# Loading the input first and the weights in six groups, with the semaphores set on ScalarE and the derived tables made in a new order

## The chip, the core and the metric

The kernel runs on one core of one Trainium2 chip. The metric is the device time of one execution in microseconds (us), and each version is timed in several runs. A core has five engines that run their own instruction streams and wait for one another through semaphores: TensorE (PE), VectorE (DVE), ScalarE (ACT), GpSimd (POOL) and SyncE (SP), which here issues every transfer between HBM and the core's memory (DMA).

## What is computed

Two transformer layers over 16 sequences of 256 tokens with 128 features. Each layer adds an attention and a feed-forward result, both taken from the same normalised input, to the running value:

```python
x = L0_attn_x
xn = _layernorm(x, axis=-1)
x = x + _L0_attn_ref(xn, ...) + _L0_ffn_ref(xn, ...)
xn = _layernorm(x, axis=-1)
x = x + _L1_attn_ref(xn, ...) + _L1_ffn_ref(xn, ...)
```

`_L0_attn_ref` is causal attention with random exponential features (16 heads of 8). `_L0_ffn_ref` is a block of depth 2 with windowed attention (8 heads of 64, rotary tables `cos`, `sin` and a scale that depends on the position), a normalisation and a gated feed-forward each. `_L1_attn_ref` is softmax attention, `_L1_ffn_ref` a mixture of 8 experts plus a shared one. Weights and biases come in as separate inputs. Some are combined before they are used: a normalisation's gain is multiplied into the first feed-forward weight `w1`, its bias is multiplied through `w1` and added to `b1`, the head scales are multiplied into the rotary tables.

## The kernel before

One program does everything. The batches are taken two at a time, so there are 8 turns (`TURNS`) of `for it in range(TURNS)` on every engine, and each turn does both layers for 512 tokens. All weights (9.7 MB) stay in the core's memory for the whole program. What lies ahead of the turns, here called the prologue, runs once, and that is all that the change touches.

The five engines' parts are written by hand in program order, and each waits with `wait_ge(semaphore, count)`. The counts of a turn start at `COUNTS[name] * (it + 1)`, so that each of the 116 semaphores in `COUNTS` is first raised by its own count: `sp.sem_inc(sem[n], COUNTS[n])` (L408), 116 instructions that stand in SP's stream ahead of its first transfer.

The prologue before the change, engine by engine:

- SP: 116 semaphore instructions (L408), then 31 weight and table transfers (L412) that all raise one semaphore, `loaded`, then the input of turn 0, `x_in` (L413).
- POOL waits for all of `loaded` (L449), then clears or fills eight tiles (L450 to L459) and counts them in `started`.
- DVE waits for `loaded` and `started` (L1256, L1257). It makes the derived tables, counted in `prep`: `fbias`, `projblk`, `sqblk`, the 16 pieces of `rot` (L1274), `apb`, the scaled `w1s` (L1282), `b1s`, three rows of `rows`, and the centred second half of `w1s` (L1291, which copies what PE made). Only then it takes the moments of the input and normalises it to `xn` (L1345 to L1359).
- PE waits for `loaded` and for DVE's memset (`prep_ps`), makes the bias products (L500, 24 instructions, and L506, 8), then multiplies the second `w1` by `center` (L511), waits for all tables (`prep` 14), and then goes into turn 0: it transposes `xn` (L520, `turn_input`), makes two value tiles (L541, `early_value`), the queries and keys (L534, `favor_query`) and the values (L549, `favor_values`). The first matmul of the loop over turns is L669.
- ACT waits for `prep` 14 and `started` 9, then copies the transposed input to `hT` and `xnT` (L1077 to L1084), the value tiles (L1089) and the scaled queries (L1103).

Of the kernel before, what the change touches and what calls it, by code (L numbers as in the profile page):

```python
# [7 lines left out]
ALU = mybir.AluOpType  # L8
ACT = mybir.ActivationFunctionType
# [54 lines left out]
    "stack_in": 26 * 16, "nm_out": 16, "nm_in": 32,  # L64
}
# [61 lines left out]
def build(nc, w, x, out):  # L127
    with ExitStack() as ctx:
# [5 lines left out]
        loaded = ctx.enter_context(nc.semaphore("weights_loaded"))  # L134
# [246 lines left out]
        def bank_of(name, k=0):  # L381
            return bank[AT[name, k][0]]
# [62 lines left out]
        N_LOADS = len(W)  # L445

        @block.gpsimd
        def _(pool):
            pool.wait_ge(loaded, 16 * N_LOADS)  # L449
# [42 lines left out]
        def _(pe):  # L492
            mm = nc.tensor.matmul
            pe.wait_ge(loaded, 16 * N_LOADS)
            pe.wait_ge(prep_ps, 1)

            for l in range(DEPTH):
                for c, (o, m) in enumerate(HC):
                    for g in range(2):
                        last = mm(bank[0][0:m, 6 * l + 2 * c + g:6 * l + 2 * c + g + 1],  # L500
                                  W["w1"][:, l, g * HID + o:g * HID + o + m], W["cols"][:, 14 + 1 + l:16 + l],
                                  start=True, stop=True)
            for i, weights in enumerate((W["fw"], W["aw"])):
                for side in range(2):
                    c = 19 + 2 * i + side
                    last = mm(bank[3][:, i * D:(i + 1) * D], W["cols"][:, c:c + 1].broadcast_to([P, P]), weights[:, 3 + side, :],  # L506
                              start=(side == 0), stop=(side == 1), skip_group_check=True)
            last.then_inc(prep_ps, 1)
            pe.wait_ge(prep, 11)
            for g in range(2):  # L510
                last = mm(bank[1 + g][:, 0:HID], W["center"][:], w1s[:, 1, g * HID:(g + 1) * HID], start=True, stop=True)  # L511
            last.then_inc(prep_ps, 1)
            pe.wait_ge(prep, 14)
            pe.wait_ge(started, 9)
            I = W["ident"]
# [55 lines left out]
            pe.wait_ge(sem["favor_qk"], COUNTS["favor_qk"] + 2)  # L571
            favor_values(0)
            for it in range(TURNS):
# [69 lines left out]
                for l in range(DEPTH):  # L643
# [166 lines left out]
                    for b in range(G):  # L810
# [443 lines left out]
        def _(dve):  # L1254
            V = nc.vector
            dve.wait_ge(loaded, 16 * N_LOADS)  # L1256
            dve.wait_ge(started, 9)  # L1257
            done = [0]

            def made(ins):  # L1260
                done[0] += 1
                ins.then_inc(prep, 1)


            V.memset(bank[0][:, 0:12], 0.0).then_inc(prep_ps, 1)
            made(V.tensor_scalar(fbias[:], W["cols"][:, 0:2], FD ** -0.5, None, ALU.mult))
            made(V.tensor_tensor(projblk[:].rearrange("p (a m) -> p a m", a=4),
                                 W["projT"].unsqueeze(1).broadcast_to([P, 4, FM]),
                                 W["block8"].rearrange("p (a m) -> p a m", a=4), ALU.mult))
            made(V.tensor_scalar(sqblk[:], W["block8"], -0.5, None, ALU.mult))  # L1270
            for l in range(DEPTH):
                for qk in range(2):
                    for i, (trig, half) in enumerate(((0, 0), (1, 1), (0, 1), (1, 0))):
                        ins = V.tensor_scalar(rot[:, l, qk, i, :], W["rotary"][:, 2 * qk + trig, :],  # L1274
                                              W["cols"][:, 2 + 4 * l + 2 * qk + half:3 + 4 * l + 2 * qk + half],
                                              None, ALU.mult)
                    made(ins)
            made(V.tensor_scalar(apb[:, 0:1], W["cols"][:, 17:18], AD ** -0.5, None, ALU.mult))
            made(V.tensor_copy(apb[:, 1:2], W["cols"][:, 18:19]))
            dve.wait_ge(prep_ps, 2)  # L1280
            for l in range(DEPTH):
                made(V.tensor_scalar(w1s[:, l, :], W["w1"][:, l, :], W["cols"][:, 10 + l:11 + l], None, ALU.mult))  # L1282
            made(V.tensor_tensor(b1s[:, :], bank[0][:, 0:12], W["b1"][:], ALU.add))
            assert done[0] == 12, done
            V.tensor_tensor(W["rows"][:, 3, :], W["rows"][:, 3, :], W["rows"][:, 6, :], ALU.add)
            for i, r in enumerate((1, 5)):
                V.tensor_tensor(W["rows"][:, r, :], bank[3][:, i * D:(i + 1) * D], W["rows"][:, r, :], ALU.add)
            made(V.memset(mv[:], 1.0))
            dve.wait_ge(prep_ps, 3)
            for g in range(2):  # L1290
                ins = V.tensor_copy(w1s[:, 1, g * HID:(g + 1) * HID], bank[1 + g][:, 0:HID])  # L1291
            made(ins)

# [76 lines left out]
            link(V.memset(ra[:, 0:TT], 1.0))  # L1370
            input_moments(0)
            link(rsqrt(2 * TT))
            input_root()
            input_scale(0)
            for it in range(TURNS):
                now, prior, freed = counters(dve, it)
                def favor_out(b):
# [16 lines left out]
                for l in range(DEPTH):  # L1394
                    for p, (qk, g) in enumerate(PAIRS):
# [340 lines left out]
```

## Time and profile before

| | |
|---|---|
| Median of three runs | 2192.03 us (2189.34 to 2197.23) |
| The profiled execution, its own time | 2193.24 us |
| Its span, first to last instruction | 2191.5 us |
| PE, DVE, ACT, POOL busy | 84%, 61%, 35%, 12% of the span |
| Mean granted TensorE clock | 0.952 |

The span is what the trace covers, and all positions below are microseconds from its start. Busy shares are averages over 8 turns and say nothing about the first 80 us, where the change lies; for these the chain of waits and the order in time are to be read. In the stretches of the prologue the page's column for the granted clock prints 1.00, whatever PE does there.

### The profile page before, as it was taken

How to read it: one execution, taken by the hardware profiler on the slowest of the kernel's cores; microseconds unless marked ns; L12 is line 12 of the kernel's file. 1: busy time of each engine (PE TensorE's matmuls, PEld its weight loads, DVE VectorE, ACT ScalarE, POOL GpSimd, SP SyncE). 2: the span in 40 equal slices, each digit the busy share in tenths (PEclk: the TensorE clock that was granted, in tenths of full speed). 3: DMA queues.
4: the chain of work that ended last, by engine and by line, in shares of the span. 5: the costliest groups of instructions: out<-in, count | busy, mean ns of one | idle time of the engine just before them, and what ended most of it. 6: DMA issues, size and time to landing. Idle time of an engine off the chain costs nothing.

```text
span 2191.5 us, 43331 instructions
## 1 busy us (share of the span) xinstructions
PE 1835.0 (84%) x18116; PEld 1061.8 (48%) x18116; DVE 1335.9 (61%) x2752; ACT 765.2 (35%) x1441; POOL 272.2 (12%) x222
## 2 busy tenths in 40 slices
PE   1698898988988889878888888888897988988887
PEld 1254454554544644536445454454553554545544
DVE  1567546765476745767547675476656675467754
ACT  0323433324533235323352232623425223433234
POOL 0101101101021010110210102101011011012010
PEclk9999999999999989999999999999999999999999
DMA  4000200002000020000200001000100002000010
GB/s 177 1 7 2 28 4 6 6 2 30 2 11 1 2 29 6 8 1 2 29 7 7 1 9 23 7 7 1 19 14 6 7 2 29 2 6 1 3 29 7
DMA packets 27477, 29.77 MB, mean 14 GB/s; under 512 B 3525, under 2 KB 25845, under 8 KB 26741
## 3 DMA queue, kind: packets, MB, share of 16 engines
q1 hardware_dynamic: 27284, 27.01, 6.3%
q8 instruction: 145, 2.38, 0.5%
q14 instruction: 48, 0.39, 0.1%
HBM read 12.06 MB, written 2.36 MB: 7 GB/s over the span
## 4 chain that ended last, share of the span: by engine, by line
PE 52%; DVE 28%; ACT 7%; issue 5%; DMA 4%; SPq 4%; POOL 0%; ACTq 0%; DVEq 0%
PE bank L957 5%; PE bank L731 5%; PE bank L947 4%; PE bank L932 4%; DMA phi<-parts 3%; SPq L430 3%; DVE ls L1455 3%; DVE ftm L1381 2%; PE bank L763 2%; PE bank L970 2%; ACT phi L1246 2%; DVE lc L1437 2%; ACT lc L1246 2%; PE bank L669 2%; DVE parts L1391 2%
## 5 line engine op out<-in xcount | busy, mean ns | idle before, releaser
L1622 DVE TENSOR_REDUCE amx<-bank 128x2 f32<-128x512 f32 x256 | 163.1, 685 | 98.4 <-PE bank L970 98.4
L1212 ACT ACTIVATE silu<-bank 128x512 f32<-128x512 f32 x144 | 84.1, 595 | 298.0 <-PE bank L932 286.0
L1610 DVE TENSOR_TENSOR mh<-bank,silu 128x512 f32<-128x512 f32 x144 | 99.5, 692 | 123.4 <-PE bank L947 115.1
L957 PEld LDWEIGHTS bank<-w_mw,mh 128*128 128x128 f32 x1152 | 145.2, 202 | 24.4 <-issue 24.4
L957 PE MATMUL bank<-w_mw,mh 128*128 128x128 f32 x1152 | 153.2, 289 | 0.0
L1641 DVE RECIPROCAL ftm<-bank 128x512 f32<-128x512 f32 x16 | 53.7, 3358 | 154.4 <-PE bank L1053 154.4
L485 POOL TENSOR_TENSOR xB<-xn2T,lsq 128x512 f32<-128x512 f32 x32 | 40.7, 1273 | 812.1 <-ACT lsq L1218 812.1
L932 PE MATMUL bank<-xn2T,w_mw 128*128 128x512 f32 x288 | 141.1, 612 | 0.0
L1455 DVE RECIPROCAL ls<-bank 128x256 f32<-128x256 f32 x64 | 112.2, 1753 | 39.7 <-PE bank L783 39.6
L1443 DVE TENSOR_REDUCE lmx<-bank 128x4 f32<-128x512 f32 x128 | 79.5, 685 | 89.4 <-PE bank L731 89.4
L669 PE MATMUL bank<-hT,w_wqkv 128*128 128x512 f32 x256 | 119.0, 602 | 11.9 <-ACT lsq L1123 6.2
L466 POOL TENSOR_TENSOR lc<-lc,ls 128x512 f32<-128x512 f32 x32 | 40.9, 1278 | 639.6 <-DVE lc L1413 639.6
L731 PE MATMUL bank<-lc 32*64 32x128 f32 (+1 forms) x3072 | 104.4, 334 | 0.0
L731 PEld LDWEIGHTS bank<-lc 32*64 32x64 f32 (+1 forms) x3072 | 78.5, 181 | 32.0 <-issue 20.3
L763 PE MATMUL bank<-lc 32*128 32x192 f32 (+1 forms) x2048 | 88.1, 308 | 0.0
L1437 DVE TENSOR_TENSOR lc<-lc,bank 128x512 f32<-128x512 f32 x128 | 79.1, 680 | 13.6 <-PE bank L712 13.6
L763 PEld LDWEIGHTS bank<-lc 32*128 32x128 f32 x2048 | 75.9, 185 | 14.5 <-issue 12.1
L1407 DVE TENSOR_TENSOR lc<-bank,rot 128x512 f32<-128x512 f32 x64 | 43.9, 687 | 60.5 <-PE bank L669 60.5
L669 PEld LDWEIGHTS bank<-hT,w_wqkv 128*128 128x128 f32 x256 | 45.4, 190 | 70.9 <-issue 44.7
L970 PE MATMUL bank<-lc,phi 48*128 48x256 bf16 x512 | 50.0, 286 | 34.1 <-DMA phi<-parts 34.1
L719 PE MATMUL bank<-w_winmask,w_ident 128*128 128x512 bf16 x128 | 47.7, 449 | 35.3 <-DVE lc L1437 14.3
L1123 ACT ACTIVATE lsq<-bank 128x512 f32<-128x512 f32 x64 | 36.5, 596 | 115.5 <-DVE ls L1410 69.2
(284 smaller groups left out, 3678.1 us busy)
## 6 DMA issues: line engine op xcount, KB each, us to landing
phi<-parts SPq DMA_DIRECT2D x96, 64.0 KB
lc<-parts SPq DMA_DIRECT2D x96, 64.0 KB
w_mw<-in_mw SPq DMA_DIRECT2D x3, 1152.0 KB
x_in<-in_x SPq DMA_DIRECT2D x8, 256.0 KB, 2.7
out<-res SPq DMA_DIRECT2D x8, 256.0 KB, 2.3
w_wqkv<-in_wqkv SPq DMA_DIRECT2D x1, 1536.0 KB
w_w<-in_w SPq DMA_DIRECT2D x1, 682.0 KB
mh<-in_rotary SPq DMA_DIRECT2D x1, 512.0 KB
```

The costliest lines, as they stand in the source:

```text
L669: mm(bank_of("loc_raw", n)[:], W["wqkv"][:, l, c * P:(c + 1) * P], h, start=True, stop=True).then_inc(sem["loc_raw_ps"], 1)
L731: ins = mm(bank_of("loc_max", k + i)[u * WIN:u * WIN + m, c0:c0 + P], lc[r, c, q0 + u * WIN:q0 + u * WIN + m], lc[r, 4 + c, k0:k0 + P], st ...
L763: mm(bank_of("loc_sT", 4 * k + i)[:, c0:c0 + nq], lc[r, 4 + c, t + kt * P:t + kt * P + P], lc[r, c, t + q0:t + q0 + nq], start=False, stop ...
L932: mm(bank_of("moe_g", n)[:], W["mw3"][:, ORDER[q], i * P:(i + 1) * P], xn2T[:], start=True, stop=True).then_inc(sem["moe_g_ps"], 1)
L947: mm(bank_of("moe_u", n)[:], W["mw1"][:, ORDER[q], i * P:(i + 1) * P], xw[q % 2] if q else xn2T[:], start=True, stop=True).then_inc(sem["m ...
L957: last = mm(bank_of("final")[:, t], mh[:, (2 * q + i) % 4, t], W["mw2"][:, ORDER[q], i, :], start=(q == 0 and j == 0 and i == 0), stop=Fal ...
L970: ins = mm(o[:, qt * SEQ:(qt + 1) * SEQ], qst[r, hh, t + qt * P:t + qt * P + P], kst[r, hh, t:t + SEQ], start=True, stop=True)
L1246: A(apr[k % 8], bank_of("att_sT", k)[:], ACT.Exp).then_inc(sem["att_p"], 1)
L1437: V.tensor_tensor(lc[:, c, :], lc[:, c, :], bank_of("loc_rb", m)[:], ALU.mult).then_inc(sem["loc_qk"], 1)
L1455: V.reciprocal(lrec[:, k % 2, :], bank_of("loc_den", k)[:, 0:SEQ]).then_inc(sem["loc_rec"], 1)
L1610: V.tensor_tensor(mh[:, n % 4, :], bank_of("moe_u", n)[:], silu[:, n % 2, :], ALU.mult).then_inc(sem["moe_h"], 1)
L1622: V.tensor_reduce(amx[:, 2 * b:2 * b + 2, h], bank_of("att_max", n)[:].rearrange("p (t k) -> p t k", t=2), AX.X, ALU.max).then_inc(sem["at ...
```

## The change

Five things change, all in the prologue.

1. `x_in` is SP's first transfer, and the weights follow in six groups, in a new order; each group raises its own semaphore (`loaded_first`, `loaded_gated`, `loaded_favor`, `loaded_local`, `loaded_tables`, `loaded_rest`). The weight `wqkv` is split into its two layers, which go into different groups.
2. Each engine waits for a group where it first needs it. POOL waits for no load at all.
3. The 116 semaphore instructions move from SP to ACT, in reversed order.
4. ACT runs one `Exp` on a single column once `started` is reached, so that its table load stands ahead of the first copy.
5. DVE normalises the input first and makes the tables after it, in a new order. PE transposes the input first and makes the bias products after it, in `bank6` instead of `bank0` and `bank3`; the centring matmul moves behind `favor_query`.

```diff
+LOADS = {
+    "first": ("ident", "cols"),
+    "gated": ("w1", "b1", "center"),
+    "favor": ("fw", "aw", "block8", "projT"),
+    "local": ("rotary", "wqkv0", "rows"),
+    "tables": ("sumrow", "causal", "sumcol", "ident4", "headrow", "winmask", "nmrow", "bandmask", "den", "mean"),
+    "rest": ("wo", "w2", "wqkv1", "wr", "rb", "pick", "rank", "mw3", "mw1", "mw2"),
 }
...
+        def arrived(group):
+            return loaded[group], 16 * len(LOADS[group])
...
-            for n in COUNTS:
-                sp.sem_inc(sem[n], COUNTS[n])
+            sp.dma_start(x_in[:], x[0]).then_inc(x_in_sem, 16)
+            for group, names in LOADS.items():
+                for n in names:
...
             sp.sem_inc(stored, 16)
-            for n, ap in w.items():
-                if n != "ones2":
-                    sp.dma_start(W[n] if n in ("rotary", "block8", "projT") else W[n][:], ap).then_inc(loaded, 16)
-            sp.dma_start(x_in[:], x[0]).then_inc(x_in_sem, 16)
...
-            pool.wait_ge(loaded, 16 * N_LOADS)
...
-            pe.wait_ge(loaded, 16 * N_LOADS)
-            pe.wait_ge(prep_ps, 1)
...
-            pe.wait_ge(prep, 14)
-            pe.wait_ge(started, 9)
...
+            def bias_products():
+                pe.wait_ge(*arrived("gated"))
+                pe.wait_ge(prep_ps, 1)
...
+                pe.wait_ge(*arrived("favor"))
...
+                last.then_inc(prep_ps, 1)
+
+            def centred_weights():
+                pe.wait_ge(prep, 5)
+                for g, o in enumerate((bank_of("xnT"), bank_of("loc_v", 0))):
+                    last = mm(o[:, 0:HID], W["center"][:], w1s[:, 1, g * HID:(g + 1) * HID], start=True, stop=True)
+                last.then_inc(prep_ps, 1)
...
+            pe.wait_ge(started, 9)
+            pe.wait_ge(*arrived("first"))
             turn_input(0)
+            bias_products()
             pe.wait_ge(sem["xnT"], COUNTS["xnT"] + 1)
+            pe.wait_ge(*arrived("local"))
             for j in range(EARLY):
                 early_value(0, j)
...
             pe.wait_ge(sem["favor_qk"], COUNTS["favor_qk"] + 2)
+            centred_weights()
             favor_values(0)
+            pe.wait_ge(prep, 13)
+            pe.wait_ge(*arrived("tables"))
...
+                    if it == 0 and l == 0:
+                        pe.wait_ge(*arrived("rest"))
                     for b in range(G):
                         n = 2 * l + b
                         pe.wait_ge(*freed("loc_wo", n))
...
-            act.wait_ge(prep, 14)
+            for n in reversed(COUNTS):
+                act.sem_inc(sem[n], COUNTS[n])
             act.wait_ge(started, 9)
+            A(warm[:], phibias[:], ACT.Exp)
...
+            act.wait_ge(prep, 1)
             queries(0)
+            act.wait_ge(prep, 13)
...
+            dve.wait_ge(prep_ps, 2)
+            dve.wait_ge(*arrived("favor"))
+            dve.wait_ge(*arrived("gated"))
+            made(V.tensor_scalar(sqblk[:], W["block8"], -0.5, None, ALU.mult))
...
+            dve.wait_ge(*arrived("local"))
+            tables(0)
...
+            tables(1)
+            dve.wait_ge(prep_ps, 3)
```

What stands in the streams, first of SP, whose rows are transfers (tile, source, shape). Before, the small tables come first and the input last:

```order
L412 DMA w_ident<-in_ident 128x128
L412 DMA w_ident4<-in_ident4 128x512
...
L412 DMA mh<-in_rotary 128x1024
...
L412 DMA w_wqkv<-in_wqkv 128x3072
...
L412 DMA w_mw2<-in_mw2 128x2304
L413 DMA x_in<-in_x 128x4x128
```

Now:

```order
L420 DMA x_in<-in_x 128x4x128
L427 DMA w_ident<-in_ident 128x128
L427 DMA w_cols<-in_cols 128x23
L427 DMA w_w1<-in_w1 128x1364
...
L427 DMA mh<-in_rotary 128x1024
L425 DMA w_wqkv<-in_wqkv 128x1536
...
L427 DMA w_mw2<-in_mw2 128x2304
```

The input moved from the 32nd place to the first, and the first half of `wqkv` and the rotary tables from the middle to places 11 and 12; the three largest weights (`mw`) still stand last.

PE at its start, before (L500 and L506 are the bias products, L511 the centring, L520 the input's transposes, L541, L534 and L549 the first products of turn 0, L669 the loop):

```order
L500 MATMUL bank0<-w_cols,w_w1 128x1 [waits bias_products,weights_loaded]
...
L506 MATMUL bank3<-w_fw,w_cols 128x128 x2
...
L511 MATMUL bank1<-w_w1,w_center 128x341 [waits vector_prepared]
...
L520 MATMUL bank2<-w_ident,xn 128x128 [waits glu_as,xn,pool_prepared,vector_prepared]
...
L541 MATMUL bank3<-w_wqkv,hT 128x512 [waits glu_gs,hT,xnT]
...
L534 MATMUL bank7<-xnT,w_fw 128x512 [waits att_mx,xnT,loc_v]
...
L549 MATMUL bank7<-w_fw,xnT 128x128 [waits att_o,favor_qk]
...
L669 MATMUL bank0<-hT,w_wqkv 128x512 [waits loc_v,favor_qk,att_p,xnT,hT]
```

And now (L535 the transposes, L515 and L522 the bias products, L556, L549 and L564 the first products, L529 the centring, L691 the loop):

```order
L535 MATMUL bank2<-w_ident,xn 128x128 [waits glu_as,xn,loaded_first,pool_prepared]
...
L515 MATMUL bank6<-w_cols,w_w1 128x1 [waits bias_products,loaded_gated]
...
L522 MATMUL bank6<-w_fw,w_cols 128x128 [waits loaded_favor]
...
L556 MATMUL bank3<-w_wqkv,hT 128x512 [waits hT,glu_gs,loaded_local,xnT]
...
L549 MATMUL bank7<-xnT,w_fw 128x512 [waits att_mx,xnT,loc_v]
...
L529 MATMUL bank2<-w_w1,w_center 128x341 [waits vector_prepared,favor_qk]
...
L564 MATMUL bank7<-w_fw,xnT 128x128 [waits att_o]
...
L691 MATMUL bank0<-hT,w_wqkv 128x512 [waits favor_qk,xnT,loc_v,hT,att_p,loaded_tables,vector_prepared]
```

The transposes moved ahead of the bias products and the centring behind the queries; the wait for all tables moved from the transposes to the loop's first matmul.

DVE at its start, before:

```order
L1265 MEMSET bank0 128x12 [waits pool_prepared,weights_loaded]
L1266 TENSOR_SCALAR fbias<-w_cols 128x2
...
L1274 TENSOR_SCALAR rot<-mh,w_cols 128x256 x16
...
L1282 TENSOR_SCALAR w_w1<-w_w1,w_cols 128x682 [waits bias_products]
...
L1291 COPY w_w1<-bank1 128x341 [waits bias_products]
L1291 COPY w_w1<-bank2 128x341
L1370 MEMSET ra 128x4
L1345 BN_STATS st_in<-x_in 128x6 [waits x_loaded,vec_step]
```

And now:

```order
L1286 MEMSET bank6 128x12 [waits pool_prepared]
L1363 MEMSET ra 128x4
L1338 BN_STATS st_in<-x_in 128x6 [waits x_loaded,loaded_first,vec_step]
...
L1352 TENSOR_SCALAR xn<-x_in,mv_in,rs_in 128x128 [waits vec_step]
...
L1389 TENSOR_SCALAR sqblk<-mh 128x128 [waits loaded_gated,loaded_favor,bias_products]
...
L1378 TENSOR_SCALAR rot<-mh,w_cols 128x256 [waits loaded_local]
L1378 TENSOR_SCALAR rot<-mh,w_cols 128x256 x7
...
L1378 TENSOR_SCALAR rot<-mh,w_cols 128x256 x8
L1405 COPY w_w1<-bank2 128x341 [waits bias_products]
L1405 COPY w_w1<-bank3 128x341
L1445 TENSOR_TENSOR lc<-bank0,rot 128x512 [waits loc_raw_ps,att_pv,vector_prepared,loaded_tables]
```

The input's statistics and scaling moved ahead of all tables, and the copies of the centred weight (L1405) stand last, just ahead of the loop's first instruction (L1445).

## Rows read from the trace of the kernel before

**Rows 1.** Core's span and mean granted clock.

```profile
core 0: 2191.5 us, clock 0.952
```

**Rows 2.** Busy time by stretch, turns 0 and 1 (PE, PEld, DVE, ACT, POOL; PEclk, DMA share, GB/s).

```profile
76.40:340.80 264.40, 228.51 (x2258) 131.49 (x2257) 162.84 (x337) 95.42 (x181) 33.44 (x26) 0.95 0.06 9
340.80:605.00 264.20, 228.23 (x2263) 131.05 (x2261) 167.82 (x341) 95.46 (x180) 33.45 (x26) 0.95 0.06 10
```

**Rows 3.** The chain that ended last, 0 to 76.5 us: start, duration, what.

```profile
25.59 15.56 DMA w_mw<-in_mw
...
41.20 0.53 POOL hT L450
...
45.77 0.09 DVE fbias L1266
...
45.99 4.69 PE bank L500 x24
50.68 1.93 PE bank L506 x8
52.63 1.07 DVE w_w L1282 x2
...
53.75 2.66 PE bank L511 x4
...
57.36 0.04 DVE ra L1370
...
62.08 1.10 PE bank L520 x4
...
63.28 1.28 ACT L1077
...
66.46 3.79 PE bank L541 x4
...
70.93 3.79 PE bank L534 x4
...
75.48 1.16 PE bank L549 x8
```

**Rows 4.** Line L408, SP's semaphore instructions: ns min/median/max, first and last start.

```profile
L408 SPq EVENT_SEMAPHORE  x116: 17/17/17, 0.7 to 7.9; - x116
```

**Rows 5.** SP's first and last transfer of the prologue, in order of time.

```profile
8.06 0.89 SPq L412 DMA_DIRECT2D w_ident<-in_ident  x2
...
26.88 0.85 SPq L413 DMA_DIRECT2D x_in<-in_x  x1
```

**Rows 6.** Busy time by stretch while the weights load (columns as in Rows 2).

```profile
8.00:16.00 8.00, 0.00 (x0) 0.00 (x0) 0.00 (x0) 0.00 (x0) 0.00 (x0) 1.00 0.47 129
...
20.00:36.00 16.00, 0.00 (x0) 0.00 (x0) 0.00 (x0) 0.00 (x0) 0.00 (x0) 1.00 1.01 407
36.00:41.00 5.00, 0.00 (x0) 0.00 (x0) 0.00 (x0) 0.00 (x0) 0.00 (x0) 1.00 0.51 192
```

**Rows 7.** Tile `x_in` in the prologue, and line L419 (later turns): issue to landing.

```profile
DMA to landing us min/median/max: 14.9/14.9/14.9
DMA to landing us min/median/max: 2.5/2.7/4.7
```

**Rows 8.** DMA packets by size from 16 to 18 us, and from 36 to 40 us.

```profile
DMA packets 111, 0.45 MB, mean 227 GB/s; under 512 B 0, under 2 KB 0, under 8 KB 111
...
DMA packets 587, 0.95 MB, mean 237 GB/s; under 512 B 31, under 2 KB 511, under 8 KB 511
```

**Rows 9.** In order of time: start, duration, engine, line, tiles.

```profile
46.18 4.29 DVE L1274 TENSOR_SCALAR rot<-mh,w_cols 128x256 f32<-128x256 f32 x16
...
76.48 1.88 PE L669 MATMUL bank<-hT,w_wqkv 128*128 128x512 f32 x4
...
80.22 3.70 PE L669 MATMUL bank<-hT,w_wqkv 128*128 128x512 f32 x8
...
137.25 1.97 PE L815 MATMUL bank<-mh,w_wo 128*128 128x256 f32 x8
```

More of the change, by code:

```diff
@@ L64 @@
     "stack_in": 26 * 16, "nm_out": 16, "nm_in": 32,
+}
+LOADS = {
[5 more added lines that the diff above has]
+    "rest": ("wo", "w2", "wqkv1", "wr", "rb", "pick", "rank", "mw3", "mw1", "mw2"),
 }
@@ L133, in build @@
         sem = {n: ctx.enter_context(nc.semaphore(n)) for n in COUNTS}
-        loaded = ctx.enter_context(nc.semaphore("weights_loaded"))
+        loaded = {g: ctx.enter_context(nc.semaphore("loaded_" + g)) for g in LOADS}
         prep = ctx.enter_context(nc.semaphore("vector_prepared"))
@@ L493, in _ @@
             mm = nc.tensor.matmul
-            pe.wait_ge(loaded, 16 * N_LOADS)
-            pe.wait_ge(prep_ps, 1)
[L497 to L511, printed above, removed]
@@ L512, in _ @@
-            last.then_inc(prep_ps, 1)
-            pe.wait_ge(prep, 14)
-            pe.wait_ge(started, 9)
-            I = W["ident"]
+            I = W["ident"]
+            def bias_products():
+                pe.wait_ge(*arrived("gated"))
+                pe.wait_ge(prep_ps, 1)
+                for l in range(DEPTH):
+                    for c, (o, m) in enumerate(HC):
+                        for g in range(2):
+                            mm(bank[6][0:m, 6 * l + 2 * c + g:6 * l + 2 * c + g + 1],
+                               W["w1"][:, l, g * HID + o:g * HID + o + m], W["cols"][:, 14 + 1 + l:16 + l],
+                               start=True, stop=True)
+                pe.wait_ge(*arrived("favor"))
+                for i, weights in enumerate((W["fw"], W["aw"])):
+                    for side in range(2):
+                        c = 19 + 2 * i + side
+                        last = mm(bank[6][:, (1 + i) * D:(2 + i) * D], W["cols"][:, c:c + 1].broadcast_to([P, P]),
+                                  weights[:, 3 + side, :], start=(side == 0), stop=(side == 1), skip_group_check=True)
+                last.then_inc(prep_ps, 1)
@@ L1255, in _ @@
             V = nc.vector
-            dve.wait_ge(loaded, 16 * N_LOADS)
             dve.wait_ge(started, 9)
[L1258 to L1292, printed above, removed]
+            V.memset(bank[6][:, 0:12], 0.0).then_inc(prep_ps, 1)
             step = [0]
@@ L1370, in _ @@
             link(V.memset(ra[:, 0:TT], 1.0))
+            dve.wait_ge(*arrived("first"))
             input_moments(0)
@@ L1374, in _, with made, tables @@
             input_scale(0)
+            done = [0]
+            def made(ins):
+                done[0] += 1
+                ins.then_inc(prep, 1)
+            def tables(l):
+                for qk in range(2):
+                    for i, (trig, half) in enumerate(((0, 0), (1, 1), (0, 1), (1, 0))):
+                        ins = V.tensor_scalar(rot[:, l, qk, i, :], W["rotary"][:, 2 * qk + trig, :],
+                                              W["cols"][:, 2 + 4 * l + 2 * qk + half:3 + 4 * l + 2 * qk + half],
+                                              None, ALU.mult)
+                    made(ins)
@@ new lines, in _ @@
+            made(V.tensor_scalar(fbias[:], W["cols"][:, 0:2], FD ** -0.5, None, ALU.mult))
+            made(V.tensor_scalar(apb[:, 0:1], W["cols"][:, 17:18], AD ** -0.5, None, ALU.mult))
+            made(V.tensor_copy(apb[:, 1:2], W["cols"][:, 18:19]))
+            dve.wait_ge(prep_ps, 2)
+            dve.wait_ge(*arrived("favor"))
+            dve.wait_ge(*arrived("gated"))
+            made(V.tensor_scalar(sqblk[:], W["block8"], -0.5, None, ALU.mult))
+            for l in (1, 0):
+                made(V.tensor_scalar(w1s[:, l, :], W["w1"][:, l, :], W["cols"][:, 10 + l:11 + l], None, ALU.mult))
@@ new lines, in _ @@
+            made(V.tensor_tensor(projblk[:].rearrange("p (a m) -> p a m", a=4),
+                                 W["projT"].unsqueeze(1).broadcast_to([P, 4, FM]),
+                                 W["block8"].rearrange("p (a m) -> p a m", a=4), ALU.mult))
+            dve.wait_ge(*arrived("local"))
+            tables(0)
+            V.tensor_tensor(b1s[:, :], bank[6][:, 0:12], W["b1"][:], ALU.add)
+            V.tensor_tensor(W["rows"][:, 3, :], W["rows"][:, 3, :], W["rows"][:, 6, :], ALU.add)
@@ new lines, in _ @@
+            for i, r in enumerate((1, 5)):
+                V.tensor_tensor(W["rows"][:, r, :], bank[6][:, (1 + i) * D:(2 + i) * D], W["rows"][:, r, :], ALU.add)
+            made(V.memset(mv[:], 1.0))
+            tables(1)
+            dve.wait_ge(prep_ps, 3)
+            for g, o in enumerate((bank_of("xnT"), bank_of("loc_v", 0))):
+                ins = V.tensor_copy(w1s[:, 1, g * HID:(g + 1) * HID], o[:, 0:HID])
+            made(ins)
+            assert done[0] == 13, done
+            dve.wait_ge(*arrived("tables"))
@@ L1375, in _ @@
             for it in range(TURNS):
                 now, prior, freed = counters(dve, it)
+                if it == 0:
+                    dve.wait_ge(prep, 13)
                 def favor_out(b):
@@ L1394, in _ @@
                 for l in range(DEPTH):
+                    if it == 0 and l == 1:
+                        dve.wait_ge(*arrived("rest"))
                     for p, (qk, g) in enumerate(PAIRS):
```

7 lines of the change are left out of this document (6 added, 1 removed).

## The prediction

> **What bounds the kernel now.** I read first the core's span and clock [rows 1], then the turns [rows 2]. Two turns take 264.4 and 264.2 us. Eight such turns are 2114 of the 2191.5 us, and no instruction of a turn is changed apart from two waits for a weight group in turn 0. So the change can only act on what lies ahead of the loop's first matmul, which starts at 76.48 [rows 9]. There the chain of waits is to be read [rows 3]: for the first 41 us it holds only SP's issue and the transfers, the last of them a `mw` weight, of the experts in the second layer. POOL's fills follow (41.20), then PE's bias products, DVE's scaling and PE's centring, then the input's normalisation (57.36), the transposes (62.08), ACT's copies with a table load (63.28), the value tiles, the queries and the loop. One engine works at a time, and each row on this chain is worth its full length. The reader is to see that the question is not how busy an engine is, but which of these rows still stand on the chain afterwards.
>
> **What starts earlier.** SP's 116 semaphore instructions run from 0.7 to 7.9 us [rows 4], and the first transfer follows at 8.06 [rows 5]; so SP can now issue at 0.7. One issue takes about (26.88 - 8.06) / 31 = 0.6 us, and 0.45 while little is queued (0.89 for two [rows 5]). `x_in` alone lands 2.5 to 4.7 us after its issue in the later turns [rows 7]: by 3.4 here, 5.4 at worst. `ident` and `cols` are issued by 1.6 and land by some 5. POOL waits for nothing and starts with the program, at about 0.7 (where L408 starts), and its fills took 45.77 - 41.20 = 4.57 us [rows 3], so DVE may start at 5.2.
>
> **The new chain, summed.**
> - POOL's fills: 0.67 + 4.57 = 5.2.
> - DVE: a memset of under 0.1, then from the memset of `ra` to PE's first transpose 62.08 - 57.36 = 4.72: 10.1.
> - PE transposes: 1.10 and a step of 0.05: 11.2.
> - PE bias products, now behind the transposes: 52.63 - 45.99 = 6.64: 17.9. ACT's copies lie beside them: from the table load's end at 63.28 + 1.28 to 66.46, 1.9 after 11.2, so 13.1. The table load (1.28) is off the chain, if ACT is ready in time (below).
> - value tiles to the end of the queries: 75.48 - 66.46 = 9.02: 26.9.
> - centring, now behind the queries: 2.66 at the pace of [rows 3]. At that place PE changed its pace before: four matmuls L541 take 3.79 [rows 3], eight L669 of the same form 3.70 a few us later [rows 9], half as long each. The granted-clock column prints 1.00 in both stretches, so I go by the durations; 2 to 1 is what its levels of 2.4 and 1.2 GHz would give. At this pace the centring is 1.3. I take 1.3, since just this row lies behind the same two steps as before: 28.2, with 29.6 as the other end.
> - DVE's two copies: from the centring's end at 53.75 + 2.66 to 57.36, about 1 us, beside `favor_values` on PE (1.16 [rows 3]): 29.4.
> The loop starts at 29.4 instead of 76.48: 47.1 us less. Gone from the chain are the wait for all loads and SP's semaphores (40.5 of it), DVE's scaling (1.07), the table load (1.28), the copies to `hT` and `xnT` (1.9), half of the centring (1.3) and the overlap of the last copies (about 1).
>
> **What I cost at nothing, and its cover.**
> DVE's tables now lie between the bias products (17.9) and the centring's end (28.2). They are 16 pieces for 4.29 us [rows 9], the scaling 1.07, and small ones (about 1.5, an estimate from 11 small instructions, most of them shorter than the 0.27 of one of the 16 pieces): 6.9 in all, done at 24.8. Behind them wait the copies, which need the centring anyway. Cover left: 3.4 us. Centring itself needs only the scaling, ready at 19.3.
> ACT's semaphore instructions: at SP's pace of 7.3 us for 116 [rows 4] they end at 8.0, the table load (1.28) at 9.3, and the first copy is wanted at 11.2, so 1.9 us is left. Queued behind them are all of ACT's copies, and every engine that waits for a semaphore raised there; `xn`, which PE needs at 10.1, is the 46th, at 3.6. ACT's own pace isn't in the trace. At twice SP's pace they end at 15.3, the copies at 18.5, and the loop loses 0.6.
> The group `local` (3.5 MB with all ahead of it) is wanted at 17.9. From 20 to 36 us the transfers ran at 407 GB/s [rows 6]; 129 GB/s from 8 to 16 us is the pace of small tables issued one by one. With `x_in` and the small ones done at 3.5, the remaining 3.2 MB take 8 us: 11.5, and the last 5 us before 41 ran at half pace, since single engines were late [rows 6]: 14.3 with that tail. Cover left: 3.6 us.
> `tables` (0.8 MB, small) by about 16, wanted at 29.4. `rest` ends where it did, less 7.4: about 34; its first user is L815 at 137.25 [rows 9], 61 us into the loop, so 90 in the new one.
>
> ACT's table load stands at 1.28 and the three copies fit into the 1.9 us behind it [rows 3], so 1.3 comes off. The Trainium skill (ScalarE: Activation LUTs, What ACT_TABLE_LOAD costs) adds a drain of 1.38 to each switch, 2.66 in all; by that the gain would be 48.4. The trace shows no such gap, though before it ACT had nothing to drain.
>
> **The base.** The profiled execution took 2193.24, 1.2 above the median of 2192.03 and inside the three runs. 2193.24 - 47.1 = 2146.1 for it, 2144.9 against the median. I give 2145.
>
> **Rivals.**
> - PE keeps its slow pace longer: centring 2.66, and the loop's first matmuls too. What was there before PE sped up is 9 us of value tiles and queries with 0.65 between them [rows 3]. The same stands there now, but what counts isn't shown. Price: 1.3 for the centring and up to 2 in the loop: 2146 to 2149.
> - PE speeds up earlier, since bias products and value tiles now follow without a gap: the queries (3.79) would take half, up to 1.9 less, and some of the value tiles: 2141 to 2144. Against it: the 6.6 us of bias products alone did not speed it up before [rows 3].
> - `local` is late. If queued transfers shared the engines instead of going in order, it would land with the last of them, 33.1 us (8.06 to 41.20 [rows 3, 5]) after a start at 0.7: at 33.8, and the loop would start 16 later: 2161. Against it: from 16 to 18 us all 111 packets were of 2 to 8 KB, and from 36 to 40 there came 511 small ones, as `x_in` has, at the very end, where it stood in the queue [rows 8]. A milder form, an engine that is late by more than 3.6 us or instruction fetches of ACT and DVE that stand behind the weights, costs 1 to 6: 2146 to 2151. The Trainium skill (Runtime: NRT & Kernel Launch, Instruction fetch mechanics) lets each engine fetch its instructions in blocks through a DMA queue of its own. By that rule ACT, with 116 instructions more ahead of its first copy, could fetch just while the weights load; no row here shows a fetch under such load, which is why the mild form has more than a token chance.
> - The groups don't help, since one engine still waits for nearly everything ahead of its first work. The first waits in each stream speak against it: POOL has none, DVE and PE begin with `first`. Price, if only SP's 7.3 us were gained: 2184.7.
> - Slower than before: the turns get longer. The granted clock is 0.952 [rows 1], so 2 x 0.048 x 2191.5 = 210 us are spent at 1.2 GHz, the lower level. The turns would begin at another phase of whatever sets this. To eat 47 us and 0.3% (6.6) more, at half a microsecond for each at the lower level, these 210 would have to become 317, a clock of 0.927. Both turns show 0.95 and differ by 0.2 us [rows 2], against the 6.7 per turn that it takes. Then 2199 or more.
>
> **How the numbers follow.** The forecast sum with its own spread of 2 either way 0.55; slow pace longer 0.15; pace earlier 0.12; late transfers or fetches, mild form 0.12; in full 0.02; groups no help 0.01; longer turns 0.01; something that none of these names 0.02, shared between faster and the rest. The range takes the first four but for their ends: 2140 to 2152. A measurement of this kernel tells about 0.3% (6.6 us) from no change. Only the longer turns and half of the unnamed case fall outside of faster: faster 0.97, same 0.015, slower 0.015.
>
> **What would show it.** In the profile after: SP's first transfer at about 0.7; POOL's fills from 0.7 to 5.2; the transposes at 10.1; the bias products right behind, to 17.9, and the value tiles without a gap (a gap released by a transfer means that `local` is late, one released by ACT that its semaphore instructions are); the queries' end at 26.9; the loop's first matmul at 29.4; turns of 264. The prediction is wrong if a turn changes by more than 1 us, if the value tiles start after 20, or if ACT reaches its first copy after 12.

## The result, and the profile after

The changed kernel takes 2139.96 us (median of four runs, 2130.53 to 2142.15) against 2191.22 for the kernel before: a ratio of 0.9761, 95% interval 0.9725 to 0.9798. That is 51.3 us less where 47.1 were forecast, and 2139.96 lies just below the range's lower end of 2140. In a later comparison on another occasion the same two kernels gave 0.9785 (0.9770 to 0.9801, 2139.53 against 2186.6, four and nine runs), 47.1 us less. Two executions among all that were timed for this document lie far outside of the rest (2649.17 and 9517.61 us), and no median or ratio given here counts them. The profiled execution of the changed kernel took 2142.15.

The core's span and mean granted clock:

```profile
core 0: 2140.4 us, clock 0.953
```

Turns 0 and 1 of the changed kernel, busy time by stretch (PE, PEld, DVE, ACT, POOL; PEclk, DMA share, GB/s), to be laid beside [rows 2]:

```profile
25.76:290.10 264.34, 228.19 (x2256) 131.20 (x2256) 163.36 (x337) 95.33 (x180) 33.41 (x26) 0.95 0.07 12
290.10:554.30 264.20, 228.41 (x2273) 131.43 (x2276) 169.11 (x344) 95.66 (x181) 33.41 (x26) 0.95 0.06 10
```

The turns are what they were. From the loop's first matmul to the end it is 2140.4 - 25.76 = 2114.6 us, before 2191.5 - 76.48 = 2115.0. All but 0.4 us of the gain lies ahead of the loop, where the chain of waits now reads (start, duration, what; beside [rows 3]):

```profile
5.26 4.32 DMA mh<-in_projT
...
10.23 1.08 PE bank L535 x4
11.32 4.35 PE bank L515 x24
15.67 1.92 PE bank L522 x8
17.59 2.30 PE bank L556 x4
...
20.56 2.00 PE bank L549 x4
...
22.58 0.70 ACT fqs L1130
...
23.32 1.43 PE bank L529 x4
...
24.78 0.94 DVE w_w L1405 x2
...
25.76 1.98 PE bank L691 x4
```

The reader sees the transposes (L535), the bias products right behind them, the value tiles (L556) without a gap, the queries (L549), the centring (L529), DVE's copies and the loop (L691). The view puts the time from 5.26 to 9.58 down to a transfer (`projT`); DVE's own rows say otherwise. In order of time, and below them the transfer of `cols`, the last of the group `first` (KB, and us from issue to landing):

```profile
5.04 0.10 POOL L472 MEMSET phibias<- 128x1 f32 x1
5.22 0.07 DVE L1286 MEMSET bank<- 128x12 f32 x1 [5.22 <-POOL phibias L472]
...
5.58 0.87 DVE L1338 BATCH_NORM_STATS2 st_in<-x_in 128x6 f32<-128x128 f32 x4 [0.23 <-DVE ra L1363]
...
8.86 1.28 ACT L1100 ACT_TABLE_LOAD   x1 [8.86 <-issue]
```

```profile
w_cols<-in_cols SPq DMA_DIRECT2D x1, 11.5 KB, 3.7
```

POOL's fills end at 5.14 and DVE starts 0.1 us later, on two memsets. Then it stands idle for 0.2 us, until its first statistics at 5.58: `cols`, issued at 1.78, lands at 5.5, and the statistics wait for it. In a second and a third profile of the same kernel (experiment 10) it took 3.4 and 3.1 us, and the statistics start at 5.39, straight behind the memsets. So fills and `cols` end at nearly the same time here, and either can be the last. From there DVE works through to `xn` (L1352). ACT has issued its 116 semaphore instructions by 8.86.

The transfer of `rows`, the last of the group `local`, KB and us from issue to landing:

```profile
w_rows<-in_rows SPq DMA_DIRECT2D x1, 448.0 KB, 7.8
```

`rows` is issued at 6.68, so `local` is complete at 14.5, 3.1 us before its first user.

### The profile page after: what moved, and what is told of

It reads as the page before. It is cut to its first block, busy times and chain, and to the rows that moved or that the text cites. A ratio compares the mean times of both kernels' runs of the same rounds, so it can differ in the third digit from the quotient of the medians.

```text
span 2140.4 us, 43336 instructions
## 1 busy us (share of the span) xinstructions
PE 1829.1 (85%) x18116; PEld 1062.6 (50%) x18116; DVE 1335.0 (62%) x2752; ACT 765.1 (36%) x1442; POOL 271.9 (13%) x222
## 3 DMA queue, kind: packets, MB, share of 16 engines
q8 instruction: 145, 2.38, 0.5%
## 4 chain that ended last, share of the span: by engine, by line
PE 52%; DVE 28%; ACT 7%; issue 4%; SPq 4%; DMA 4%; ACTq 0%; DVEq 0%
PE bank L981 5%; PE bank L753 5%; SPq L446 4%; PE bank L971 4%; PE bank L956 4%; DMA phi<-parts 3%; DVE ls L1493 3%; DVE ftm L1417 3%; PE bank L785 3%; ACT phi L1275 2%; PE bank L994 2%; DVE parts L1427 2%; ACT lc L1275 2%; DVE lc L1475 2%; PE bank L691 2%
## 5 line engine op out<-in xcount | busy, mean ns | idle before, releaser
L691 PE MATMUL bank<-hT,w_wqkv 128*128 128x512 f32 x256 | 119.1, 603 | 12.1 <-ACT lsq L1152 6.2
L785 PEld LDWEIGHTS bank<-lc 32*128 32x128 f32 x2048 | 75.9, 185 | 14.5 <-issue 12.1
L691 PEld LDWEIGHTS bank<-hT,w_wqkv 128*128 128x128 f32 x256 | 45.4, 190 | 71.2 <-issue 44.5
L741 PE MATMUL bank<-w_winmask,w_ident 128*128 128x512 bf16 x128 | 47.0, 444 | 35.7 <-DVE lc L1475 14.5
L956 PEld LDWEIGHTS bank<-xn2T,w_mw 128*128 128x128 f32 x288 | 50.9, 193 | 53.1 <-issue 51.8
```

Source lines behind the costliest of these rows:

```text
L691: mm(bank_of("loc_raw", n)[:], W["wqkv"][:, l, c * P:(c + 1) * P], h, start=True, stop=True).then_inc(sem["loc_raw_ps"], 1)
L785: mm(bank_of("loc_sT", 4 * k + i)[:, c0:c0 + nq], lc[r, 4 + c, t + kt * P:t + kt * P + P], lc[r, c, t + q0:t + q0 + nq], start=False, stop ...
L956: mm(bank_of("moe_g", n)[:], W["mw3"][:, ORDER[q], i * P:(i + 1) * P], xn2T[:], start=True, stop=True).then_inc(sem["moe_g_ps"], 1)
```

## The experiments

Where the loop starts can be read to 0.1 us in a profile, while the time of an execution wanders: from the loop's first matmul to the end the profiles below give 2107 to 2121 us for one and the same code. So parts of a few microseconds are told by the loop's start, and the time only where a difference is large. All edits are to the changed kernel unless said otherwise.

**1. Semaphores back on SP.**

```diff
-            for n in reversed(COUNTS):
-                act.sem_inc(sem[n], COUNTS[n])
...
+            for n in COUNTS:
+                sp.sem_inc(sem[n], COUNTS[n])
             sp.dma_start(x_in[:], x[0]).then_inc(x_in_sem, 16)
```

> The changed kernel with the 116 semaphore instructions back on SP, ahead of its first transfer. In the changed kernel the loop over turns starts at 25.76 us, DVE's first statistics at 5.58 and the local group has about 5 us of cover. Theory (only what ends last counts): x_in is issued at about 8.1 and lands 2.5 to 2.7 later, ident and cols at about 11, so DVE starts at about 11.2 and the loop at 31.4 (5.6 later), not 7.3 later, since POOL's fills cover the first 5.2 us. Rival (each microsecond of SP counts in full): loop at 33.1.

2154.73 us in one run; the loop starts at 32.30, 6.5 later. The row of DVE's first statistics, in order of time, with its wait in brackets:

```profile
12.05 0.87 DVE L1338 BATCH_NORM_STATS2 st_in<-x_in 128x6 f32<-128x128 f32 x4 [6.69 <-DMA w_cols<-in_cols]
```

DVE's statistics start at 12.05, 6.5 after 5.58, and everything behind them moves by as much. It is neither the 5.6 of the theory nor the 7.3 of the rival. `cols`, 11.5 KB, lands last of the three, 2.9 us after its issue at 9.06. That issue is 7.3 later than in the changed kernel, where `cols` took 3.7 us and was waited for as well: between these two profiles the difference of 0.8 is the landing's own spread, and POOL's fills cover none of it. Against the two other profiles of the changed kernel, in which the fills do end last (5.39), it is 6.7, so the cover of the fills is about 0.6 us and not the 1.7 of the theory.

**2. One semaphore for all groups.**

```diff
-        loaded = {g: ctx.enter_context(nc.semaphore("loaded_" + g)) for g in LOADS}
+        loaded_all = ctx.enter_context(nc.semaphore("loaded_all"))
+        loaded = {g: loaded_all for g in LOADS}
...
-            return loaded[group], 16 * len(LOADS[group])
+            return loaded_all, 16 * sum(len(v) for v in LOADS.values())
```

> The changed kernel with one semaphore for all six groups, so that each wait for a group is a wait for all weights; order of transfers, ACT's semaphores and the new order of the work are kept, and POOL and x_in are free. Theory (the groups are worth what lies between the first and the last landing): DVE starts when all has landed, at about 28.5 to 29 instead of 5.58, the loop at 49, 23 later, and the time is about 2163. Rival (the gain came from the input first and from SP and POOL, the groups add nothing): loop within 2 us of 25.8.

2159.80 us, 0.9868 (0.9838 to 0.9898) of the kernel before. The chain of waits, start and duration:

```profile
5.36 24.46 issue
29.82 0.88 DVE st_in L1339 x4
...
49.89 1.98 PE bank L692 x4
```

DVE stands for 24.5 us and the loop starts at 49.89, 24.1 later. So the groups carry about half of the gain. The rest is left to the earlier first transfer, POOL's freedom and the new order; experiments 5 and 6 price the first two in the kernel before.

**3. All bias products ahead of the transposes.**

```diff
-            turn_input(0)
             bias_products()
+            turn_input(0)
```

> The changed kernel with PE's bias products ahead of the input's transposes, as in the kernel before. Work is the same, but the value tiles now stand behind a pause in which ACT copies the input. Theory A (PE's pace rises because its work runs on without a pause from the bias products into the value tiles): with the pause the pace rises only late in the queries, as before, and the loop starts at about 28. Theory B (a pause of 2 us doesn't matter for the pace, only the order of the chain does): bias products from about 6.7, transposes at about 13.1, value tiles at about 16.1, pace rising at or before 18.5, loop at 24 to 25.

2136.97 us in one run; the loop starts at 26.77. The chain of waits:

```profile
7.72 4.69 PE bank L515 x24
12.42 1.92 PE bank L522 x8
14.33 0.87 PE bank L535 x4
...
17.11 3.79 PE bank L556 x4
...
21.57 2.00 PE bank L549 x4
```

Neither theory held in full. PE now pauses for 1.9 us (15.20 to 17.11) while ACT copies. The value tiles start 0.5 earlier than in the changed kernel, not 1.5, since the first product waited for `center` until 7.72. And they take 3.79, the slow pace, against 2.30, while the queries are fast.

**4. The group `rest` ahead of `local` and `tables`.** In `LOADS` the line `"rest"` moves up in front of `"local"`.

> The changed kernel with the group rest (5.1 MB) ahead of local and tables in SP's queue. Theory (queued transfers are served in order): local lands with the last 1.7 MB, at about 25 to 26, the value tiles start there instead of at 17.59, PE has lost its pace by then, and the loop starts at 36 to 38. Rival (queued transfers share the engines, so that order matters little): value tiles before 20, loop before 29.

2151.45 us in one run. The chain of waits:

```profile
17.40 10.25 issue
27.64 3.77 PE bank L556 x4
...
32.08 3.79 PE bank L549 x4
...
36.64 2.64 PE bank L529 x4
```

PE stands 10.2 us for `local`, which was ready at 14.5 when it was queued ahead. Transfers of this queue are served in their order. The loop starts at 40.45, later than the expected 36 to 38: `local` landed 1.6 us or more after the expected 25 to 26, and value tiles, queries and centring all ran at the slow pace. In a second profile of the same kernel (experiment 10) the value tiles start at 27.13 and take 3.77 again, the queries take 2.00, and the loop starts at 36.78.

**5. Before, with ACT's semaphores alone.** In the kernel before, the same 116 instructions go from SP to ACT.

> The kernel before with one part of the change alone: the 116 semaphore instructions on ACT, in reversed order. ACT is idle until 63 us there. Theory (the chain's first piece is SP's): every transfer starts 7.3 us earlier and so does all behind it: the loop starts at 69.2 instead of 76.48, time about 2184. Rival (the last of 9.7 MB lands when the engines have moved it, and the first 8 us of issue are hidden behind that): loop at 74 or later.

2177.45 us (median of five), 0.9943 (0.9922 to 0.9964). The first profile is of the execution of 9517.61 us, in which PE was some three times slower from its first product on (14.00 us for the 24 products instead of 4.69), so PE's positions in it tell nothing; a second profile was taken.

> The kernel before with ACT's semaphores alone, again, for its profile: the first profile was of an execution in which PE ran several times slower than in all others. There the last weight landed at 32.05 instead of 41.20. Theory (issue on SP sets all of the load's time up to its queue's end): the last weight lands 7.3 to 9.2 earlier and the loop starts at 67.3 to 69.2. Rival (landing hidden behind the engines' total): loop at 74 or later.

```profile
15.31 16.02 DMA w_mw<-in_mw
31.38 0.53 POOL hT L448
...
56.62 3.79 PE bank L539 x4
...
61.08 2.00 PE bank L532 x4
```

The last weight lands at 31.38, 9.8 us earlier than in [rows 3] and 7.6 earlier than in the third profile of the kernel before (38.97, experiment 10); in the first profile of this run it landed at 32.05. The 7.3 of the instructions lies near the lower end; how much of the rest is the landing's own spread isn't told. The loop starts at 64.84, 11.6 earlier than in [rows 3], 1.8 of it from queries at the fast pace.

**6. Before, with POOL free of the loads.** In the kernel before, `pool.wait_ge(loaded, 16 * N_LOADS)` is left out.

> The kernel before with POOL's wait for the weights left out, so that its fills run while the weights load. Theory (the fills are on the chain for their full 4.57 us): the loop starts at 71.9 instead of 76.48. Rival: at 76, since PE and DVE find another wait.

2184.70 us in one run; the loop starts at 69.36, 7.1 earlier than in [rows 3]. The chain of waits:

```profile
5.21 33.44 issue
38.65 0.10 DVE fbias L1265
...
59.34 3.80 PE bank L540 x4
...
63.81 3.79 PE bank L533 x4
```

DVE starts straight at the last landing. The 4.57 of the fills are gone; the other 2.6 us come from a landing at 38.65 instead of 41.20.

**7. Without ACT's early Exp.** `A(warm[:], phibias[:], ACT.Exp)` is left out.

> The changed kernel without ACT's early Exp; its Exp in the first turn loads the table where needed. My prediction counted the table load (1.28 us) as taken off the chain. Theory (it is the new order that hides it: ACT's copies end at 13.2 and are wanted at 17.6, behind the bias products): loop start unchanged within 0.3 us of 25.8, or later by about 1.3 if the load of the Exp table then falls between the queries and the loop. Rival (the early Exp is what takes it off): value tiles 1.3 later, at 18.9.

2142.06 us in one run. ACT's table load, in order of time, and the value tiles in the chain of waits:

```profile
11.22 1.28 ACT L1103 ACT_TABLE_LOAD   x1 [11.22 <-PE bank L535]
```

```profile
17.41 3.43 PE bank L556 x4
```

The value tiles start at 17.41, as with it (17.59, 17.40 and 17.39 in the three profiles of the changed kernel). The table load now stands ahead of ACT's first copy, and no second one follows before the loop; the copies end at 14.35, 3.1 us before they are wanted. The Exp is worth nothing: the new order had already put ACT's copies beside the bias products. The loop starts at 26.71, 0.95 later, all of it in the pace of the value tiles. In both profiles without the Exp these took 3.43, in three with it 2.30 to 3.09; whether that is more than the spread isn't settled.

**8. Three extra matmuls ahead of the transposes.** Their result isn't used.

```diff
+            z = avz[:].rearrange("p j a e -> p (j a e)")
+            for i in range(3):
+                mm(bank[0][:], z[:, 128 * i:128 * i + 128], z[:, 512:1024], start=True, stop=True)
             pe.wait_ge(*arrived("first"))
             turn_input(0)
```

> The changed kernel with three extra matmuls of 128x512 f32 from POOL's filled tile into a bank that is free, on PE from 5.3 us, while PE waits for the input (to 10.2); their result isn't used. Theory (PE's pace rises after some microseconds of matmul work, whatever the work): three take about 5.1 us, the pace rises by the bias products or the transposes instead of at 18.5, and 24 products of 0.19, the 8 and the value tiles shrink: loop at 21.5 to 24. Rival (the pace rises at a point that doesn't hang on earlier work, or bias products with one column are bound by something else): loop at 25.8 or, if the extra ones end after 10.2, later.

2139.99 us, 0.9758 (0.9731 to 0.9784), as without them. The loop starts at 28.26, 2.5 later. The chain of waits, and below it the stretches (columns as above, before and after PE's clock column fell):

```profile
5.20 5.49 PE bank L582 x6
10.68 0.64 PE bank L535 x4
11.32 2.29 PE bank L515 x24
13.61 1.10 PE bank L522 x8
...
15.32 3.76 PE bank L556 x4
...
19.76 3.79 PE bank L549 x4
...
24.32 2.64 PE bank L529 x4
```

```profile
11.00:14.40 3.40, 3.40 (x35) 3.40 (x33) 0.00 (x0) 1.78 (x3) 0.00 (x0) 1.00 1.02 382
14.40:16.00 1.60, 0.99 (x3) 0.51 (x3) 1.25 (x4) 0.00 (x0) 0.00 (x0) 0.50 1.14 338
```

The theory's first half is right: behind the extra matmuls the 24 products take 2.29 instead of 4.35, and the 8 take 1.10 instead of 1.92. But then the granted clock is 0.50, that is 1.2 GHz, from 14.4 on, and value tiles, queries and centring all run at it. In the 3.40 us before the fall PE had been busy for 100% by the page's count: with the last 0.3 us of the transposes, then the 24 one-column products (2.29), then most of the 8 products of 128 columns. So the page's busy share of PE doesn't tell whether the pace will hold. It is one profile, and which of these products let the pace go isn't shown. By the theory the loop would have started at 21.5 to 24; the fall was in neither expectation.

**9. The 24 one-column products ahead of the transposes, the 8 behind them.**

```diff
+            bias_columns()
             turn_input(0)
-            bias_products()
+            bias_rows()
```

> The changed kernel with the 24 one-column bias products ahead of the input's transposes (PE is idle there, from about 7.7 us in the run with all bias products first) and the 8 others behind them, beside ACT's copies. Theory (the bias products were on the chain for 6.3 us, of which all but the 1.9 beside ACT's copies can be moved into PE's idle time): value tiles at about 15.3 instead of 17.59; the loop 2.3 earlier than with the changed kernel at the same point of the pace's rise, so between 23.3 and 26. Rival (the rise of PE's pace hangs on work without a pause, so it comes later and eats this): loop at 25.8 or later. The time itself moves by 0.1%, below what timing tells.

2135.07 us, 0.9773 (0.9752 to 0.9793) of the kernel before; the changed kernel has 0.9785 (0.9770 to 0.9801) in the same comparison, so timing can't tell them apart. The chain of waits:

```profile
7.66 4.69 PE bank L515 x24
12.35 0.97 PE bank L537 x4
...
15.22 2.87 PE bank L558 x4
...
18.77 2.00 PE bank L551 x4
...
23.97 1.98 PE bank L694 x4
```

The value tiles start 2.4 earlier and the loop at 23.97, 1.6 to 2.4 earlier than in the three profiles of the changed kernel. It is the shortest prologue of all versions here.

**10. The same kernels again.** The pace was the term that had failed, and it differed between profiles with one and the same PE order. So unchanged kernels were profiled again.

> The changed kernel once more, unchanged. In its first profile PE's pace rose 0.9 us after the value tiles' start; in the run without ACT's Exp, whose PE order is the same, 4.3 after. Theory (the point varies from execution to execution by some microseconds, whatever the kernel): another point than 18.4, between 18 and 22, loop start between 25.7 and 28. Rival (the kernel sets it): 18.4 and 25.76 again within 0.3.

> As after_2: a third profile of the changed kernel. By the theory of variation the pace's rise falls elsewhere between 18 and 22; by the rival again at 18.4.

> The kernel before, unchanged, for a second profile. Theory (a pause of PE ahead of the value tiles puts the rise of its pace off): the queries' four matmuls take 3.79 in full or nearly, rise 4 to 12 us after the value tiles' start. Rival (chance): any point from 0.8 on. It also shows how far the last weight's landing, 41.20 in the first profile, moves by itself (38 to 42).

> The kernel before, a third profile, with the same two expectations.

> The changed kernel with the group rest ahead of local and tables, again: PE pauses for 10 us ahead of the value tiles. Theory: rise 4 to 12 us after their start. Rival: any point, also below 4.

> The changed kernel without ACT's early Exp, again; no pause of PE ahead of the value tiles. Theory: rise 0.8 to 4.2 us after their start, value tiles' start at 17.4 again (that is what tells of the Exp), loop at 25.6 to 26.8. Rival: rise later than 4.2 in some profile.

The changed kernel's value tiles took 3.09 and 2.33, its loop started at 26.36 and 25.59: the second profile differs from the first by 0.6 us, the third by 0.2 only. Without the Exp the second profile repeats the first (value tiles from 17.40, 3.43; loop at 26.70). The expectation for the kernel before and for `rest` first, queries slow in full or nearly, failed in all three repeats. In the third profile of the kernel before, the chain of waits has:

```profile
38.97 0.53 POOL hT L450
...
64.21 3.67 PE bank L541 x4
...
68.55 2.00 PE bank L534 x4
```

Here the last weight landed at 38.97 and the queries ran fast, against the expectation; the loop started at 72.31 instead of 76.48, in the second profile at 74.42 (landing 40.95, queries 2.00). The 1.9 us in the chain of experiment 9 are no pause of PE: the 8 products lie beside ACT's copies, and PE's own row shows an idle time of 0.21 us in brackets.

```profile
15.22 2.86 PE L558 MATMUL bank<-w_wqkv,hT 128*128 128x512 f32 x4 [0.21 <-ACT xnT L1114]
```

Laid together, by what PE did ahead of the value tiles (four matmuls each: 3.79 all slow, 2.00 all fast):

| PE ahead of the value tiles | value tiles, us | queries, us |
|---|---|---|
| pause of over 3 us (before, before_2, before_3, b_pool_early, b_sems_on_act_2, rest_first, rest_first_2) | 3.79, 3.80, 3.67, 3.80, 3.79, 3.77, 3.77 | 3.79, 2.00, 2.00, 3.79, 2.00, 3.79, 2.00 |
| pause of 1.9 us (bias_first) | 3.79 | 2.00 |
| pause of 0.2 us (split_bias) | 2.87 | 2.00 |
| no pause (after, after_2, after_3, no_exp, no_exp_2, one_wait, sems_on_sp) | 2.30, 3.09, 2.33, 3.43, 3.43, 2.19, 2.38 | 2.00 in all seven |

With a pause of 1.9 us or more the value tiles took 3.67 to 3.80, with one of 0.2 us or none 2.19 to 3.43. The two don't overlap, though only 0.24 us lie between them. (The run with the extra matmuls stands apart: its pace had risen and fallen again.) The closest pair is rest_first against the changed kernel: the same products ahead, and the pause alone is new. So a pause puts the rise off, and within a group its point still moves from one execution to the next: the value tiles of one kernel differ by 0.8 us (2.30 to 3.09), the queries of another by their whole 1.79. The second profile of rest_first was taken on another chip than the first, so for its queries chance and chip aren't told apart.

## Why the prediction was nearly right, and where it failed

- **What bounds the kernel, and that only the prologue moves.** Right: the two turns differ by under 0.1 us from those before, all that follows the loop's start by 0.4.
- **SP, POOL, DVE.** Forecast: fills end at 5.2, transposes at 10.1. Measured: DVE's first memset at 5.22, the transposes at 10.23, the first transfer at 0.73. The 0.2 us that DVE stood for `cols` had no term; in the two other profiles, without them, the transposes start at 10.04.
- **Bias products.** Forecast 6.64 to 17.9; measured 4.35 + 1.92 = 6.27, to 17.59. The first of them overlap the transposes' end.
- **Value tiles to the end of the queries, 9.02: this step failed.** It was taken over from [rows 3], where both run at the slow pace. Measured: from 17.59 to 23.32, 5.7. The value tiles took 2.30 and the queries 2.00 where 3.79 each was counted: 3.3 of the 3.6 us between the forecast 29.4 and the measured 25.76. The rival that named it ("PE speeds up earlier, since bias products and value tiles now follow without a gap", 2141 to 2144) was given 0.12; its argument was right, as the table shows, and the counter-argument was not. That the bias products alone did not speed PE up before is true, and in experiment 8 a fast pace even fell behind them; but work ahead without a pause brings the rise forward all the same. The Trainium skill (TensorE: Matmul & The Clock Gate, Part 1) has the throttled state as the default and lets activity release it. The trace agrees as far as a pause costs pace; what counts as activity, the busy share of experiment 8 (3.40 of 3.40 us, then 0.50) does not tell.
- **The row itself was a poor base.** 3.79 for the queries is one of three profiles of the kernel before; the two others have 2.00. One profiled execution gives a duration that depends on such a state only once.
- **Centring.** Forecast 1.3 at the fast pace, measured 1.43. Copies beside `favor_values` to the loop: about 1, measured 0.98.
- **What was costed at nothing.** `local` was ready at 14.5, against 14.3 forecast, and `rest` at some 30 instead of 34, with no effect. DVE's tables were ready at 23.9, only 0.9 us ahead of its last copies (24.78) where 3.4 of cover were counted, since the centring ended 3.4 us earlier than forecast and the tables only 0.9. ACT's semaphore instructions took (8.86 - 0.7) / 116 = 70 ns each instead of 63, an estimate that takes their start from SP's, and with the Exp's own 0.20 they left 1.0 us of cover instead of 1.9. No wait for an instruction fetch stands on the chain. Crediting 1.28 to the table load was right as a sum over the chain, but it is the order that hides it and not the early Exp (experiment 7). The drain that the Trainium skill (ScalarE: Activation LUTs, What ACT_TABLE_LOAD costs) adds does not show here either: the load is from 8.86 to 10.14 and the Exp starts at 10.15; nothing ran on ACT ahead of it.
- **Order of service.** Right, and shown by experiment 4. "The groups don't help" is refuted by experiment 2, "longer turns" by the turns themselves.
- **The base.** The forecast gain was taken from one profile whose loop starts at 76.48; three profiles give 76.48, 74.42 and 72.31, mean 74.4, and three of the changed kernel 25.76, 26.36, 25.59, mean 25.9. The difference of the means is 48.5. The 51.3 of the first comparison and the 47.1 of the later one lie to its two sides. That the later one equals the forecast gain is luck: the forecast start of the loop, 29.4, was 3.0 to 3.8 us too late in all three profiles, and the base of 76.48 about 2 too late as well. The range of 12 us had no room for this wandering of the base, besides the pace.

What stays open: what sets the point at which PE's pace rises. Eight profiles with a pause of 1.9 us or more and eight with 0.2 us or none show that a pause puts it off; whether the one-column products ahead help or only don't hurt was not told apart, and why the pace fell in experiment 8 isn't known.

## What to carry to other kernels

Ahead of a loop, follow the chain and ask of each wait for loads which transfer it needs; queue those first and wait for them alone. Splitting the wait was worth 24 us at the loop's start here, and moving semaphore instructions from ahead of the first transfer to an idle engine 6.5 to 6.7. Before a PE duration from a start-up phase goes into a sum, look whether the same form runs twice as fast a little later: such a row holds for its history of pauses and not for the instruction. And where a gain is a few microseconds, read it at a position in several profiles, and not from the time.

## What the runs showed of the hardware that was not expected

- One-column f32 products follow PE's pace as well: 24 of them take 4.35 to 4.69 us or 2.29.
- With PE busy 3.40 of 3.40 us, 2.29 of it on them, the granted clock still fell to 0.50 (experiment 8, one profile).
- The granted-clock column prints 1.00 in stretches of the prologue where the durations show the slow pace (3.79 for the four matmuls L541 of the kernel before, whose form later takes half as long), so there the durations are the only witness.
- 11.5 KB (`cols`), third in the queue, took 3.7, 3.4 and 3.1 us from issue to landing in three profiles of the changed kernel.
- The landing of the last of 9.7 MB moved between 38.65 and 41.20 us over four profiles with the same queue.
